# Three box-filter layers: 128-partition loads in the outer two, a table of distances and one channel of all images a step in the middle one

## The reference

```python
z = bn1(einsum('kc,bchw->bkhw', w1, x))            # 64 -> 16 channels, per pixel
S = integral image of z (cumsum over rows and columns)
box = (F11 - F10 - F01 + F00) / area               # four bilinear samples of S, boxes of x_min..x_max, y_min..y_max
out = relu(x + relu(bn2(box)))                     # 64 channels again
```

## Time and profile before

| | |
|---|---|
| median of 3 runs | 3755.85 us (3750.78 to 3760.55) |
| the profiled execution's own time | 3755.65 us |
| its span (first to last instruction) | 3753.8 us |
| granted TensorE clock, mean | 0.954 of full speed |
| busy over the span | PE 88%, DVE 65%, ACT 63%, POOL 46% |
| DMA | 334.15 MB, mean 89 GB/s |

### The profile page before, as it was taken

One profiled execution on the slowest core, in us unless ns is written; L12 is line 12 of the kernel. 1 busy time (PEld: TensorE's weight loads), 2 busy tenths in 40 slices (PEclk: granted clock), 3 DMA queues, 4 the chain that ended last, 5 costly groups with the idle time before them and its releaser, 6 DMA issues. The chain is left out here.

```text
span 3753.8 us, 54069 instructions
## 1 busy us (share of the span) xinstructions
PE 3297.6 (88%) x18664; PEld 2007.8 (53%) x18664; DVE 2439.5 (65%) x4175; ACT 2375.8 (63%) x3944; POOL 1713.8 (46%) x1397
## 2 busy tenths in 40 slices
PE   3953789999999999998989999999999999787479
PEld 0742555556564646464646464655556565254247
DVE  2845666767676766666666767676767655269467
ACT  0854566767676767676766666666767666557358
POOL 2404554555555454554545454554545532144232
PEclk9985999999999999999999999999999999989779
DMA  9871110111111110313111111110111111263798
GB/s 235 252 256 58 45 62 34 57 46 46 51 46 56 36 62 29 118 60 124 59 68 40 51 40 51 46 59 33 62 43 48 51 40 61 77 245 121 193 257 242
DMA packets 233725, 334.15 MB, mean 89 GB/s; under 512 B 37616, under 2 KB 162160, under 8 KB 227328
## 3 DMA queue, kind: packets, MB, share of 16 engines
q1 hardware_dynamic: 198112, 298.44, 23.6%
q10 hardware_dynamic: 27392, 18.44, 2.1%
q0 software_dynamic: 7968, 13.99, 1.5%
HBM read 183.99 MB, written 146.80 MB: 88 GB/s over the span
## 5 line engine op out<-in xcount | busy, mean ns | idle before, releaser
L1511 ACT ACTIVATE a_hidden<-a_wide,a_up_b 128x1024 f32<-128x1024 f32 x512 | 568.7, 1111 | 138.9 <-PE a_wide L1690 137.5
L1690 PE MATMUL a_wide<-a_yc,a_up_fold 64*128 64x512 f32 x2048 | 585.0, 647 | 44.1 <-ACT a_hidden L1511 39.8
L1701 PE MATMUL a_result<-a_hidden,a_down 128*64 128x512 f32 x2048 | 508.5, 618 | 38.3 <-ACT a_hidden L1511 33.8
L1259 POOL TENSOR_TENSOR a_y<-a_o,a_mag 128x256 f32<-128x256 f32 (+1 forms) x512 | 365.3, 738 | 385.9 <-DVE a_mag L1354 385.9
L1217 POOL TENSOR_TENSOR a_y<-a_x,a_stat 128x512 f32<-128x512 f32 x256 | 267.7, 1046 | 556.7 <-DVEq L1399 540.1
L1337 DVE TENSOR_TENSOR a_o<-a_bank,a_mix_b 128x512 f32<-128x512 f32 (+1 forms) x272 | 181.5, 667 | 278.0 <-PE a_bank L1647 272.4
L1665 PEld LDWEIGHTS a_bank<-a_dft_h,a_g 128*128 128x128 f32 x2080 | 272.4, 191 | 128.9 <-issue 128.9
L1647 PEld LDWEIGHTS a_bank<-a_mix,a_o 128*128 128x128 f32 x2080 | 252.8, 191 | 150.8 <-issue 132.8
L1524 ACT ACTIVATE a_delta<-a_result,a_down_b 128x512 f32<-128x512 f32 x256 | 175.8, 687 | 236.9 <-PE a_result L1701 236.9
L1384 DVE TENSOR_REDUCE a_stat<-a_sq 128x16 f32<-128x1024 f32 x240 | 290.8, 1211 | 31.4 <-ACT a_sq L1545 29.9
L1365 DVE TENSOR_TENSOR a_x<-a_result,a_x 128x512 f32<-128x512 f32 x256 | 175.9, 687 | 203.3 <-PE a_result L1716 202.6
(11 more groups left out here) (191 smaller groups left out, 6440.3 us busy)
## 6 DMA issues: line engine op xcount, KB each, us to landing
a_x<-rows SPq DMA_DIRECT2D x112, 512.0 KB, 4.4
rows<-a_x SPq DMA_DIRECT2D x112, 512.0 KB, 2.7
box_x<-in_x SPq DMA_DIRECT2D x64, 256.0 KB, 4.3
turned<-box_o SPq DMA_DIRECT2D x64, 256.0 KB, 3.6
a_y<-turned SPq DMA_DIRECT2D x16, 1024.0 KB, 10.4
box_x<-rows SPq DMA_DIRECT2D x16, 1024.0 KB, 24.7
turned<-box_work SPq DMA_DIRECT2D x64, 256.0 KB, 2.0
box_x<-turned SPq DMA_DIRECT2D x64, 256.0 KB, 4.0
```

Source lines behind the costliest of these rows:

```text
L1259: ins = G.tensor_tensor(y[n % 2][:, :, to].rearrange("p c k -> p k c"), o2[:, j % 3, lo:4, r], mask[:, lo:4], ALU.mult)
L1511: A(hidden[:, i % 2, j], wide[:], ACT.Gelu, bias=up_b2[:, l, j:j + 1]).then_inc(s_hid, 1)
L1690: mm = M(wide[:, half * BANK:(half + 1) * BANK], up_fold[cs, l, j * P:(j + 1) * P], yc[cs, i % 2], start=True, stop=True)
L1701: mm = M(result[half * C:(half + 1) * C, :], down[:, l, j, :], hidden[:, i % 2, j, half * BANK:(half + 1) * BANK], start=j == 0, stop=j == ...
```

## The change

**Outer layers (`box_layer`, first and third).** A unit is now one 1 MB load over 128 partitions, issued by SP alone: partition 2c + h holds half h of channel c, where before c and 64 + c held the halves. ACT issues no unit loads. The two loads of `w1` (elements of 4 bytes, 64 x 16 each) move from SP, where they stood ahead of the units, to ACT behind the `bn1c` loads; they go to every second partition of a zeroed tile, so that the product with 1/sqrt(var) is one instruction. The input of the third layer is now stored channel first (`planes`, [B, C, P, P]) and no longer row first (`turned`): a unit's run in DRAM grows from 512 B to 8 KB, and a residual load's run shrinks from 2 KB to 512 B.

**Middle layer (`box_rows`).** (1) The taps: for each of 128 pairs of axis and channel, one row of 255 values over all distances is computed once, in three kinds of DVE instructions (`make_table`), and stored to DRAM (`table`). The taps of a group are two 256 KB loads from it by SP; partition p reads 128 values from column p on. `make_raw` and `make_taps` go. The image rows are put into reverse order in the head (`reverse`, and h counted down), so that the column index rises with the partition. (2) The order of the second sum: PE first makes the first sums of all four images of a group (`first`, one group ahead), and step s = channel c then takes the second taps of that one channel over all four images: one product 128x512 in place of four 128x128, and one ACT instruction in place of four. (3) z in DRAM is [B, P, K, P] for this layer, stored in runs of 512 B where they were 2 KB. (4) The output of a step is one channel of four images, in runs of 512 B, where it was four channels of one image in runs of 2 KB. (5) `second_bn` runs inside the head and not ahead of it; `ident` is loaded first by SP and not last by POOL.

```diff
 box_layer, SP:
-                    sp.dma_start(xc[0:C, t % RING, :].rearrange("c (p q) -> c p q", q=P),
-                                 src["half"](b, 0)[:, j * U_ROWS:(j + 1) * U_ROWS, :]).then_inc(s_unit[t % RING], 16)
+                    sp.dma_start(xc[:, t % RING, :], src["halves"](b)[:, j * U_ROWS * P:(j + 1) * U_ROWS * P]
+                                 ).then_inc(s_unit[t % RING], 16)
...
-                    for h in range(2):
-                        sp.dma_start(w1t[h * C:(h + 1) * C, :], w["w1"].rearrange("k c -> c k")).then_inc(s_par1, 16)
 box_layer, ACT:
-                for t in range(RING):
-                    load_upper(t)
+                    act.wait_ge(s_w1_zero, 1)
+                    for h in range(2):
+                        act.dma_start(w1t[h:P:2, h, :], w["w1"].rearrange("k c -> c k")).then_inc(s_w1_ld, 16)
...
 box_rows, SP:
+                def load_taps(k):
+                    for a in range(2):
+                        first = table[a * C + k * NB:a * C + (k + 1) * NB, :]
+                        stretch = bass.AP(first.tensor, first.offset, [[1, P], [2 * P, NB], [1, P]])
+                        sp.dma_start(taps[:, k % 4, a], stretch).then_inc(s_taps[k % 4], 16)
+
+                sp.wait_ge(s_table_out, 16)
+                for k in range(4):
+                    load_taps(k)
...
-                    if b == 0 and 3 <= k + 2 < K:
+                    if n == 0 and 3 <= k + 2 < K:
                         sp.wait_ge(s_f1, B * k)
                         load_z(k + 2)
+                    if n == 1 and 4 <= k + 3 < K:
+                        sp.wait_ge(s_f2, NB * k)
+                        load_taps(k + 3)
                     sp.wait_ge(s_relu, s + 1)
-                    sp.dma_start(dst(b)[:, k * NB:(k + 1) * NB, :], o[:, s % 4]).then_inc(s_out[s % 4], 16)
+                    sp.dma_start(dst(s), o[:, s % 4].rearrange("p (b i) -> p b i", b=B)).then_inc(s_out[s % 4], 16)
 box_rows, POOL:
-                    to = zd[b].rearrange("k (g j r) q -> g j k (r q)", g=UNITS // B, j=8)[g]
+                    to = zd[b].rearrange("(g r j) k q -> g (j k) r q", g=UNITS // B, j=8)[g]
...
+                pool.wait_ge(s_table, 1)
+                pool.dma_start(table[:, 0:2 * P - 1], ramps[:, 0]).then_inc(s_table_out, 16)
 box_rows, DVE:
+                def make_table():
+                    dve.wait_ge(s_par, par_before + 16 * N_PAR[layer])
...
+                    for m in range(2):
+                        ins = V.tensor_scalar(ramps[:, m], line[:], ends[:, m:m + 1], None, ALU.add)
...
+                    V.tensor_scalar(ramps[:], ramps[:], 0.0, 1.0, ALU.max, ALU.min).then_inc(s_ramp, 1)
...
+                    V.tensor_tensor(ramps[:, 0], ramps[:, 0], ramps[:, 1], ALU.subtract).then_inc(s_table, 1)
...
-                    res = x[:, b, :, k * NB:(k + 1) * NB].rearrange("p h n -> p n h")
-                    V.tensor_tensor(summed[:, s % 2], pre[:, s % 2], res, ALU.add).then_inc(s_sum, 1)
-                    if b < 2 and 3 <= k + 2 < K:
-                        make_taps(k + 2, b)
+                    V.tensor_tensor(summed[:, s % 2], pre[:, s % 2], x[:, :, :, s].rearrange("p b h -> p (b h)"), ALU.add
+                                    ).then_inc(s_sum, 1)
 box_rows, ACT:
-                    for n in range(NB):
-                        c = k * NB + n
-                        ins = nc.scalar.activation(pre[:, s % 2, n], banks[2 + s % 3][:, n * P:(n + 1) * P], ACT.Relu,
-                                                   bias=bias2[:, c:c + 1], scale=scale2[:, c:c + 1])
+                    nc.scalar.activation(pre[:, s % 2], banks[2 + s % 3][:], ACT.Relu, bias=bias2[:, s:s + 1],
+                                         scale=scale2[:, s:s + 1]).then_inc(s_pre, 1)
 box_rows, PE:
-                    for j in range(NB):
-                        mm = nc.tensor.matmul(banks[2 + s % 3][:, j * P:(j + 1) * P], taps[:, k % 3, 1, j, :],
-                                              half1[:, s % 2, j, :], start=True, stop=True)
+                    nc.tensor.matmul(banks[2 + s % 3][:], taps[:, k % 4, 1, n, :],
+                                     half1[:, k % 2, n].rearrange("p b i -> p (b i)"), start=True, stop=True
+                                     ).then_inc(s_f2, 1)
...
-                first(0)
+                for f in range(B):
+                    first(f)
                 for s in range(STEPS):
-                    if s + 1 < STEPS:
-                        first(s + 1)
+                    if s + B < STEPS:
+                        first(s + B)
                     second(s)
 build:
-    turned = [scratch(f"turned{i}", [B, P, C, P]) for i in range(3)]
+    turned, planes = scratch("turned", [B, P, C, P]), scratch("planes", [B, C, P, P])
+    table = scratch("table", [P, 2 * P])
+    def channels_first(t):
+        return {"pcq": lambda b: t[b].rearrange("c p q -> p c q"),
+                "halves": lambda b: t[b].rearrange("c (s p) q -> (c s) (p q)", s=2)}
```

209 lines of the change are left out of this document (94 added, 115 removed).

## The result

The changed kernel takes 3671.13 us (median of four runs, 3670.3 to 3674.28) against 3755.56 us of the kernel before, a ratio of 0.9777 (95% interval 0.9760 to 0.9794). It is faster, and 3673 was predicted.

The account below looks back on a forecast made before the run. Bounds taken: DMA in the outer heads, PE in outer steps, DVE with POOL beside it in middle steps. First head -20, third head -20, third steps +2, middle head +2, middle steps -46: -82 from 3755.65, 3673 us; range 3648 to 3708.

Parts of the forecast that it names:

- First layer's head, -20: Before the first layer's steps: net gain of 20 us from unit loads and moved w1 elements, bounds 9.5 to 27.
- Together -20.6 us: First layer's unit loads: 20.97 MB in 50.2 us instead of 66.4, plus 4.4 us from the slow last half loads.
- gives about as much back: First layer's head: units no longer queuing behind the w1 elements regains about the 8 us that idle time costs.
- some 8 us: First layer's head: cost of the engines idling from about 30 to 38 us while w1 elements delay the first product.
- the first step near 72.5: First layer: first step at about 72.5 us instead of 92.99, the remaining loads and stores taking 32.6 us.
- head -20 and steps +2: Third layer: head gains 20 us like the first layer's; short residual runs add 2 us to steps, mostly hidden by PE.
- Middle steps, -45.8: Middle layer's 64 steps: PE binds at 1.72 us each, 122 us in all with start, end and gaps, from 167.8.
- Middle head, +2: Before the middle layer's steps: second_bn's stall and tap loads queued behind image loads cost 2 us, between -2 and +8.
- Tap loads, 1.1 us: Middle layer's steps: each 256 KB load of overlapping, unaligned table rows takes 1.1 us, hidden if like the other transfers.
- The rival in which they bind: Tap loads bind the middle steps: 3717 us total at 3 us each, 3690 at 2, centre 3700; chance 0.12.
- Rate of the heads, 418 GB/s: Outer heads: unit loads over 128 partitions with z stores beside them run at 418 GB/s, as in the middle head before.
- The rival of 367: Outer heads reach only 367 GB/s, 57.1 us in place of 50.2, 7 a head, 3687 us total; chance 0.09.

Follow-up runs that it names:

- w1_first: The changed kernel with the two loads of w1 back on SP's queue, ahead of the units; 3654.22 us, ratio 0.9723 to the kernel before.
- middle_only: The changed middle layer with the outer layers of the kernel before, the third reading a channel-first source; 3706.12 us, ratio 0.9861.
- best1: The changed kernel with w1 by rows in all three layers, eight zs buffers for four, an outer layer's first two raws made by DVE; 3652.39 us.
- old_taps_work: The changed kernel with the old POOL and DVE work on the taps added into a tile nobody reads; 3719.23 us, ratio 0.9902.
- pool_busy: The changed kernel with two unused POOL additions for every group of four middle-layer steps; 3676.52 us, ratio 0.9789.
- units_ahead: As best1, but the rows of w1, ident and bn1r moved from SP's queue to ACT's; 3681.78 us, ratio 0.9801.

## Why the prediction was right

The sum is 2 to 3 us off, and part of that is luck. The outer layers gained less than forecast (35.1 us in the profile, against 38), the middle one more (47.2 against 43.8), and 2.4 us lie in the Fourier blocks.

*First layer's head, -20; measured -18.8 for the layer (-21.0 to -22.3 in six profiles of the same code).* The net is right by luck, since two of its parts are not right. The step that failed is the pair "Together -20.6 us" for the unit loads and, of the `w1` elements, "gives about as much back". The loads alone are worth 27.2 and 27.4 us a layer (w1_first against middle_only, which have `w1` in the same place), and moving `w1` to ACT costs 14 to 21 us in both layers together (windows of w1_first against the seven profiles with `w1` on ACT), 7 to 11 a layer. So the idle time's price of "some 8 us" was right, and that it comes back was wrong. The two errors cancel. The loads were under-sized because 316 GB/s of the earlier trace rows was taken for the whole head. Other windows of before say otherwise:

```profile
20.00:30.00 10.00, 3.81 (x16) 0.43 (x16) 1.97 (x9) 0.20 (x1) 0.64 (x1) 1.00 1.02 293
...
60.00:80.00 20.00, 3.87 (x16) 0.40 (x16) 3.84 (x5) 2.06 (x3) 3.36 (x5) 1.00 1.02 251
80.00:90.00 10.00, 3.87 (x16) 0.40 (x16) 1.96 (x3) 0.10 (x1) 0.60 (x1) 1.00 1.00 229
```

The mean from 20 to 90 us is about 281 GB/s, and 20.97 MB at 281 and at 418 are 74.6 and 50.2 us: 24.4 with the tail in it. That the first product comes at 34 us (34.34), that the engines idle from 30 to 38 (31 to 37.5), that elements pass one for one (up to 25 us), and the first step near 72.5 (71.75) all held. The 72.5 has 1.9 us that the sum doesn't name, since 38 and 32.6 are 70.6. What was not seen is that the steps do not start in full at the first step: z of later images is late. POOL's additions, 3.75 us for two, stand between its stores of z. One DVE instruction beside them took 7.40 us for 64 elements a partition:

```profile
45.20 0.75 DVE L362 TENSOR_SCALAR box_zs<-box_bank,box_bias 128x512 f32<-128x512 f32 x1 [5.36 <-DMA z<-box_zs]
45.87 7.40 DVE L343 TENSOR_SCALAR box_t<-box_bn 128x64 f32<-128x64 f32 x1
```

best1 removes both and gains nothing, so it is the arrival of the data that counts and not this path.

*Third layer, head -20 and steps +2; measured -16.3 (up to -19.7 in other profiles).* The head gave 24 at the first step and 8 went in the next four. Behind them the steps cost 0, not +2: the DMA share rose to 0.92 to 0.96, but PE covers it.

*Middle steps, -45.8; measured 122.1 us for the steps (3320.75 to 3442.89) against the 122 of the sum.* Step 1.71 (1.72), PE full, DVE 86% (near 85). Three small terms are off and cancel. The slow start costs 2.5 us and not 3.5: five products in 6.77 us, where 0.86 each is 4.3. (The record of 2.07 us in the earlier trace rows is one product in two parts, and not two products.) Gaps are 1.3 us and not 3. The end is 8.3 us and not 5.4 (PE's last product ends at 3434.6), since DVE has three more additions to do when PE stops. Mis-sized and without effect: ACT's merged instruction is 0.777 us and not 0.69; it reads a scale from a tile besides the bias that L747 has. ACT then has 1.37 us a step and stays below 1.72. Had ACT been the bound, that would have been the error. The claim that DVE "with the taps, and POOL beside it" set the old step is shown by old_taps_work.

*Middle head, +2; measured -1.5* (first step 73.8 us after the layer's start, 75.3 before), inside its -2 to +8.

*Tap loads, 1.1 us; measured 0.98.* The rival in which they bind starts where seven transfers exceed 6.88 us: 0.93 x 5 + 2T, T = 1.1 us. The chosen value lay on that edge, and the measured one leaves 0.3 us a group. It was closer than its chance of 0.12 said.

*Rate of the heads, 418 GB/s: held in part.* In the changed kernel's first head it is 379 and 389 beside the elements, 381 from 40 to 60 us and 419 from 60 to 65; the sign "heads at over 400 GB/s" is met only at the end. w1_first has 422 from 20 to 40 us. The rival of 367 lies below all of these, and is out. The 358 GB/s a core that the Trainium skill gives for HBM (DMA: Bandwidth & Descriptors, Where 436 GB/s comes from) is exceeded here too, with loads and stores counted together.

## What to carry to other kernels

In this kernel parameters in many small elements did best ahead of the big loads on the same queue, or as rows; beside the loads on another queue they get one packet for one, and the whole start waits. Read a head's rate in every stretch of it, not in one window. And for what an engine needs per step take its busy time in a window over the steps in it, not the sum of median durations, which counts overlapped time twice for short ACT instructions (2.46 against 1.94 us).

## What was not expected of the hardware

- 256 KB loads with runs of 512 B at unaligned, overlapping places cost 0.98 us, and 0.78 when every partition reads an aligned row of its own.
- From 20 to 40 us of the first layer, halves of 64 partitions move at 239 GB/s on one queue and 304 on two, and full width at 422, each at a DMA share of 1.02 to 1.03. The share doesn't show the difference; only GB/s does.
- POOL's additions on SBUF cost DVE about half of their own time: 10.3 us for 21.1 (pool_busy).
- In best1 the DMA engines are nearly idle between 5 and 10 us (share 0.10, then 0.47) although unit loads have been issued since 3.5 us. From 5 to 7.5 us SP's queue passes 165 packets with 0.01 MB in all, the parameter rows that stand ahead of the units. units_ahead, which has them on ACT's queue, has a share of 1.00 from 5 to 10 us, but loses more by what it delays. So the rows ahead hold the units; why 165 small packets take that long was not settled.
